# A two-phase attention and expert kernel on one core: one block in place of two, the first expert's weights loaded during the last attention, and a new order of GpSimd's pieces

## The chip, the cores and the metric

One core of a Trainium2 chip (trn2) runs the whole program. The metric is the device time of one execution in microseconds (us); the profile's span runs from the first to the last instruction of one profiled execution. The engines are TensorE (PE, its weight load PEld), VectorE (DVE), ScalarE (ACT), GpSimd (POOL) and SyncE (SP). SP, ACT and POOL issue DMAs.

## What is computed

x and ctx are 8 batches of 512 tokens with 256 features. In short:

```python
x = x + tanh(g_xattn) * cross_attention(layernorm(x), ctx, ctx)      # 16 heads of 16
u = layernorm(x)
h = u + attention(rmsnorm(u, g1), wq, wk, wv, wo)                    # causal, rotary
logits = rmsnorm(h, g2) @ w_router                                   # 8 experts, best 2 of each token
moe = sum over the 2 experts e: weight_e * (silu(r @ wg[e]) * (r @ wu[e])) @ wd[e]   # r = rmsnorm(h, g2), hidden 704
x = x + tanh(g_ffn) * (h + moe)
```

## The kernel before, in words

The program has two blocks, each with an instruction list for every engine. All engines leave the first before any begins the second.

**The first block** does both attentions of all batches and the routing. Its work is a list of 16 units (L60), a cross or an own (causal) attention of one batch, each in four groups of four heads. It is written as steps -1 to 7 (LAST is 7); a step has eight stages of 16 PE units, 128 PE units in all. In a unit of stage s, PE computes one tile of scores for the row maxima (`max_unit`, L645), one tile for the exponentials of the group before (`key_unit`, L665), and products with the values. DVE reduces the maxima (L981). At the end of a stage POOL splits the group's negated maxima into three bf16 parts (`split_neg`, L1298 on; its operations are L1305 to L1308), PE turns them in the middle of the next stage (`neg_turn`, L710), ACT sends them into the stack of queries, and the exponentials wait for that. So POOL is late when the split of a stage is not done by the middle of the next one.

Tables at L142 to L178 say at which PE unit (`at(step, unit)`) or POOL stage (`stage(step, s)`) all the rest happens: the rows of x and ctx, projections, rotary terms (`rotate`, POOL, L1315 on), the rows of h (DVE, L1112), their squares (ACT, L920), `hn2_rows` (POOL, L1344), which PE turns for the router (`turn("hn2", ...)`, L729), `choose` and `place` on DVE (L1033 to L1082), `base_rows` (POOL, L1351 and L1352: the residual with its gate, which SP stores into the output) and `scatter` (POOL, L1372 and L1374: four indirect DMAs for each of the two experts k, which put 128 rows each into `rows_in`, ordered by expert). Both scatters of a batch send the same buffer `hn2[b % 2]`, whose last column is rewritten between them, so the second waits until the first has landed. POOL also splits the experts' weights into high and low parts, in 64 pieces of 256 to 704 columns (`split_piece`, L1278 to L1282, eight for each expert), as many in each stage as `PIECES_IN_STEP` says; in a stage all but the last piece, then `hn2_rows` and `base_rows`, come ahead of `split_neg`, and the scatters and the last piece behind it.

```python
for b, k in due(ROTATE_STAGES, now): rotate(b, k)
...
for n in pieces_in(now)[:-1]: split_piece(n)
for b, _ in due(HN2_STAGE, now): hn2_rows(b)
for b, _ in due(BASE_STAGE, now): base_rows(b)
if ng: split_neg(step, ng)
...
for b, k in due(SCATTER_STAGES, now): scatter(b, k)
for n in pieces_in(now)[-1:]: split_piece(n)
```

At the end DVE makes a table (`table`, L1156 to L1187) with the expert, the first row and the weight offset of each of 71 tiles, SP stores a tile of padding behind each expert's rows (L632, eight DMAs), and SP and POOL wait until everything has landed.

**The second block** has its own buffers (L1431 on). SP loads expert 0 and, when it has landed, expert 1 (`load_expert`, L1477 and L1478, about 4.2 MB each, in four DMAs); expert e comes when expert e - 2 is used up. For each of 71 tiles of 128 rows ACT loads the rows (L1569), PE turns them (L1611), ACT and DVE make high and low parts (L1576, L1527), PE multiplies (L1634), ACT and DVE do silu and product (L1587, L1546 to L1549), PE turns that (L1647) and multiplies again (L1658), DVE scales (L1536) and POOL adds the rows into the output with an indirect DMA (L1502).

Of the kernel before, what the change touches and what calls it, by code (L numbers as in the profile page):

```python
# [13 lines left out]

# [16 lines left out]
HG = 4  # L31
# [103 lines left out]
def stage(i, s):  # L135
# [9 lines left out]
X1_SUMS = {b: at(b - 2, 124, 128) for b in BATCHES} | {0: at(-1, 112, 114), 1: at(0, 46, 48), LAST: at(LAST - 2, 112, 114)}  # L145
# [27 lines left out]
BASE_STAGE = {b: stage(b + 1, 5) for b in BATCHES} | {LAST - 1: stage(LAST, 1), LAST: stage(LAST, 5)}  # L173
SCATTER_STAGES = {b: (stage(b + 2, 5), stage(b + 2, 6)) for b in BATCHES} | \
    {LAST - 4: (stage(LAST - 2, 2), stage(LAST - 2, 3)), LAST - 3: (stage(LAST - 1, 2), stage(LAST - 1, 3)),
     LAST - 2: (stage(LAST - 1, 7), stage(LAST, 0)), LAST - 1: (stage(LAST, 4),) * 2, LAST: (stage(LAST, 7),) * 2}
PIECES_IN_STEP = {-1: (0, 0, 1, 1, 1, 1, 1, 1), 0: (2, 0, 0, 0, 1, 2, 2, 1), LAST - 2: (0, 0, 1, 2, 1, 0, 1, 1),
                  LAST - 1: (2, 0, 0, 3, 3, 2, 1, 1), LAST: (0,) * 8}  # L178
# [93 lines left out]
def flamingo_block(nc, x, ctx, g_xattn, g_ffn, wq, wk, wv, wo, w_router, wg, wu, wd, g1, g2, out):  # L272
# [25 lines left out]
    with outer:  # L298
# [23 lines left out]
        with ExitStack() as st:  # L322
# [3 lines left out]
            squares_sb = s1("squares_sb", 5, P)  # L326
# [8 lines left out]
            q_stack = [s1(f"q_stack{g}", HG, S, dt=BF16) for g in range(G)]  # L335
            k_stack = [s1(f"k_stack{g}", HG, S, dt=BF16) for g in range(G)]
            probs = s1("probs", 2, HG, S)
            v_of = {"cross": s1("v_cross", QT, H, 32), "own": s1("v_own", QT, H, 32)}
            x_in, ctx_in = s1("x_in", QT, D), s1("ctx_in", QT, D)
# [3 lines left out]
            hn1_t, flat_q, flat_k = s1("hn1_t", DC, S), s1("flat_q", DC, S), s1("flat_k", DC, S)  # L343
            turned = {"q": s1("turned_q", DC, S), "k": s1("turned_k", DC, S)}
            with_cos = {"q": s1("with_cos_q", DC, S), "k": s1("with_cos_k", DC, S)}
            rest = s1("rest", DC, S)
            parts = {"q": s1("parts_q", 3, DC, S, dt=BF16), "k": s1("parts_k", 3, DC, S, dt=BF16)}
            out_t = s1("out_t", S)
            own_t = s1("own_t", DC, S)
            kept = s1("kept_sb", 2, QT, D)  # L350
            h = s1("h", QT, D)
# [12 lines left out]
            sq, ss = s1("sq", D), s1("ss", QT)  # L364
# [9 lines left out]
            def bank(name, dt=F32, n=512):  # L374
# [16 lines left out]
                rank_r route scat tab_ld pad_at pad""".split()  # L391
# [53 lines left out]
            def values_read(eng, which, b):  # L445

                u = UNIT_OF[which, b]
                users = [n for n, unit in enumerate(UNITS[:u]) if value_tile(*unit) == value_tile(which, b)]
                if users:
                    eng.wait_ge(m["pv_mm"], (users[-1] + 1) * (G * 16))  # L450

# [3 lines left out]
            def _(sp):  # L455
# [58 lines left out]
                def load_kept(b):  # L514
                    sp.wait_ge(m["kept_st"], (b + 1) * 32)
                    over(sp, m["h_base"], b)
# [23 lines left out]
                def body(step):  # L540
# [96 lines left out]
                sp.wait_ge(m["ld_pad"], 16 * SPARE)  # L637


            @block.tensor  # L640
            def _(pe):
# [209 lines left out]
                run_steps(pe, body)  # L851


            @block.scalar
            def _(act):
# [100 lines left out]
                run_steps(act, body)  # L956


            @block.vector
            def _(dve):  # L960
                v = nc.vector
                chain = Chain(dve, m["dve"])
                v.memset(count[:, :], 0.0)
# [91 lines left out]
                def place(b, c):  # L1055
# [18 lines left out]
                    if c == 2:  # L1074
# [4 lines left out]
                        v.tensor_copy(hn2[b % 2][:, :, D:D + 1], token[:, :].rearrange("p (t e) -> p t e", e=1))  # L1079
# [61 lines left out]
                def table(v, chain):  # L1141
# [33 lines left out]

                    link(v.tensor_tensor(among, wide(full_f), passed, ALU.mult))
# [49 lines left out]
            def _(pool):  # L1226
# [467 lines left out]
```

## Time and profile before

| | us |
|---|---|
| three runs, median (lowest to highest) | 1619.45 (1614.07 to 1620.33) |
| the profiled execution's own time | 1617.12 |
| its span | 1614.5 |
| PE busy | 1441.7 (89% of the span) |
| DVE busy | 978.8 (61%) |
| POOL busy | 879.8 (54%) |
| ACT busy | 776.8 (48%) |

The share of busy time is a mean over two stages that differ. It has to be read by stretches, and at each idle stretch of PE by what ended it. A number in square brackets in a row of the timeline is the time for which the engine sat idle before that row, with what ended it.

### The profile page before, as it was taken

To read this page: it belongs to the slowest core of one execution; us is meant where nothing else is said; L and a number is where in the kernel's file an instruction comes from. 1 tells how busy PE (TensorE), PEld (TensorE's weight loads), DVE (VectorE), ACT (ScalarE), POOL (GpSimd) and SP (SyncE) were. 2 spreads that over 40 slices of the span, in tenths; PEclk is the share of its full clock that TensorE was granted. 3 is DMA by queue.
4 is the path that set the end of the run, shared out by engine and by line. 5 is a ranking of instruction groups with operands and counts; after the bars stand their busy time and mean duration, and the time that the engine had idled before them with its cause. 6 is when DMAs were issued, how large, how long until landed. Compare 5 with 4: busy or idle time off the path is not lost. (4 is left out here: it accounts for less than half of the span.)

```text
span 1614.5 us, 31714 instructions
## 1 busy us (share of the span) xinstructions
PE 1441.7 (89%) x9439; PEld 885.6 (55%) x9439; DVE 978.8 (61%) x2328; ACT 776.8 (48%) x1781; POOL 879.8 (54%) x1146
## 2 busy tenths in 40 slices
PE   3999999999999999999997997841999999999997
PEld 1232334444444444444444454431899999999996
DVE  5887757658757767757755654332555555555554
ACT  1566665665664665664664554610333333333332
POOL 7475765874876867975777686541122222222222
PEclk9899999999998999999998998955999999999999
DMA  7665365663564566564453556116343543455221
GB/s 204 175 173 176 95 187 163 177 203 117 178 205 149 157 187 190 150 224 134 141 162 98 196 147 212 55 65 238 83 138 50 147 135 86 115 148 148 40 41 14
DMA packets 116517, 230.19 MB, mean 143 GB/s; under 512 B 20101, under 2 KB 82949, under 8 KB 114310
## 3 DMA queue, kind: packets, MB, share of 16 engines
q1 hardware_dynamic: 76690, 148.18, 30.5%
q0 software_dynamic: 26032, 69.82, 15.4%
q10 hardware_dynamic: 13636, 10.18, 2.4%
q8 instruction: 86, 1.41, 0.4%
q14 instruction: 73, 0.60, 0.1%
HBM read 135.10 MB, written 93.14 MB: 141 GB/s over the span
## 5 line engine op out<-in xcount | busy, mean ns | idle before, releaser
L981 DVE TENSOR_REDUCE neg<-max_ps 128x1 f32<-128x512 f32 (+3 forms) x864 | 544.1, 666 | 304.3 <-PE max_ps L662 197.5
L867 ACT ACTIVATE probs<-key_ps 128x512 f32<-128x512 f32 (+3 forms) x1024 | 497.2, 519 | 388.5 <-PE key_ps L679 192.0
L659 PE MATMUL max_ps<-k_stack,q_stack 96*128 96x512 bf16 (+3 forms) x1024 | 360.0, 355 | 35.2 <-DVE neg L981 21.3
L676 PE MATMUL key_ps<-q_stack,k_stack 99*128 99x512 bf16 (+3 forms) x1024 | 355.5, 348 | 25.1 <-ACT probs L867 16.5
L1502 POOL DMA_INDIRECT out<-part,whose x71 | 110.7, 1559 | 390.1 <-DVE part L1536 328.7
L1634 PE MATMUL up_ps<-weights,rows_t 128*128 x1278 | 292.5, 383 | 5.8 <-DMA weights<-w_split 4.8
L1634 PEld LDWEIGHTS up_ps<-weights,rows_t 128*128 128x128 f32 x1278 | 233.4, 190 | 44.3 <-issue 6.4
L659 PEld LDWEIGHTS max_ps<-k_stack,q_stack 96*128 96x128 bf16 x1024 | 101.7, 99 | 224.0 <-DVE neg L981 116.2
L676 PEld LDWEIGHTS key_ps<-q_stack,k_stack 99*128 99x128 bf16 x1024 | 101.0, 99 | 131.4 <-ACT probs L867 69.1
L1658 PE MATMUL y_ps<-weights,hidden_t 128*128 x1207 | 160.7, 287 | 1.4 <-DVE hidden_t L1556 1.4
L1658 PEld LDWEIGHTS y_ps<-weights,hidden_t 128*128 128x128 f32 x1207 | 147.7, 189 | 1.7 <-issue 1.7
L697 PE MATMUL pv_ps<-probs,v_cross 128*32 128x512 f32 (+3 forms) x1024 | 132.4, 588 | 3.4 <-ACT out_t L937 2.3
L1597 ACT ACTIVATE hidden_t<-hid_ps 128x512 fp32r<-128x512 f32 (+1 forms) x142 | 61.9, 488 | 134.2 <-PE hid_ps L1647 134.2
L1587 ACT ACTIVATE silu<-up_ps 128x512 f32<-128x512 f32 (+1 forms) x142 | 66.0, 465 | 112.0 <-PE up_ps L1634 112.0
L1305 POOL TENSOR_SCALAR neg_parts<-neg 128x16 bf16<-128x16 f32 x64 | 16.2, 253 | 180.4 <-DVE neg L981 155.0
L679 PE MATMUL key_ps<-squares_b 128*128 128x128 bf16 x512 | 114.5, 224 | 0.0
L662 PE MATMUL max_ps<-squares_b 128*128 128x128 bf16 x512 | 113.4, 221 | 0.0
L697 PE MATMUL pv_ps<-probs,v_own 128*32 128x512 f32 (+3 forms) x1024 | 103.5, 473 | 3.1 <-ACT out_t L937 2.0
L1546 DVE TENSOR_TENSOR hidden<-silu,up_ps 128x320 f32<-128x320 f32 x71 | 34.6, 488 | 101.1 <-ACT silu L1587 101.1
L1576 ACT ACTIVATE rows_t<-rows_ps,g_sb 128x128 fp32r<-128x128 f32 x142 | 44.3, 363 | 103.9 <-PE rows_ps L1611 103.9
L1279 POOL TENSOR_TENSOR w_parts<-w_in,w_parts 128x704 fp32r<-128x704 f32 (+2 forms) x64 | 85.9, 1343 | 5.4
L1556 DVE TENSOR_TENSOR hidden_t<-hid_ps,hidden_t 128x512 fp32r<-128x512 f32 x71 | 49.1, 692 | 45.4 <-ACT hidden_t L1597 45.4
(202 smaller groups left out, 1966.0 us busy)
## 6 DMA issues: line engine op xcount, KB each, us to landing
w_split<-w_parts POOLq DMA_DIRECT2D x32, 704.0 KB, 5.6
weights<-w_split SPq DMA_DIRECT2D x8, 2816.0 KB
weights<-w_split SPq DMA_DIRECT2D x8, 1280.0 KB
rows<-rows_in ACTq DMA_DIRECT2D x71, 129.0 KB, 2.1
w_split<-w_parts POOLq DMA_DIRECT2D x16, 512.0 KB, 3.5
kept_sb<-kept SPq DMA_DIRECT2D x16, 512.0 KB, 6.2
parts_cross_k<-parts_k SPq DMA_DIRECT2D x48, 128.0 KB
parts_cross_q<-parts_q SPq DMA_DIRECT2D x48, 128.0 KB
```

What stands on the lines that cost most here:

```text
L659: r = mm(ps[:, 0:keys], q_stack[g][0:KROWS, hd, qt * P:(qt + 1) * P], k_stack[g][0:KROWS, hd, 0:keys], start=True, stop=not own)
L662: r = mm(ps[:, qt * P:keys], ident_b, mask_qk, start=False, stop=True)
L676: r = mm(ps[:, q0:S], k_stack[g][0:KROWS + NEGROWS, hd, kt * P:(kt + 1) * P], q_stack[g][0:KROWS + NEGROWS, hd, q0:S], start=True, stop=no ...
L679: r = mm(ps[:, q0:q0 + P], ident_b, mask_kq, start=False, stop=True)
L697: mm(pv_ps[32 * hd:32 * hd + 32, q0:S], v_of[value_tile(which, b)][:, kt, g * HG + hd, :], probs[:, kt % 2, hd, q0:S], start=(kt == 0), st ...
L867: act.activation(probs[:, kt % 2, hd, q0:S], key_ps[j % 2][:, q0:S], ACT.Exp).then_inc(m["exp_done"], 1)
L981: v.tensor_reduce(neg[:, g % 2, hd - place_:hd + 1, qt], scores, op=ALU.max, axis=AX.X, negate=True).then_inc(m["max_red"], many)
L1279: chain.link(g_.tensor_tensor(low, whole, high, ALU.subtract))
L1502: g_.indirect_dma_start(out=out_rows, out_offset=bass.IndirectOffsetOnAxis(ap=whose[j % OWNERS][:, 0:1], axis=0), in_=part[j % OWNERS][:, ...
L1587: act.activation(silu[:, f0:f1], chunk(j, k)[:, 0:f1 - f0], ACT.Silu).then_inc(m["silu"], 1)
L1634: r = mm(ps, rows_t[:, a, c, :], weights[:, bass.ds(off + (w_ * WALL + c * 2 * F + n0), n1 - n0)], start=(c == 0 and (a, w_) == PASSES[0]) ...
L1658: r = mm(y_ps[:, 0:D], hidden_t[:, a, k, :], weights[:, bass.ds(off + (w_ * WALL + 2 * WG + k * D), D)], start=(k == 0 and (a, w_) == PASS ...
```

## The change

- **One block.** The second block's work is made by `expert_stage()` inside the first, with the same loops; each engine goes on to it when its own list is done. Its buffers lie over attention buffers that are no longer used: the weights' two halves over the stacks, x_in, ctx_in, v_cross, flat_q and parts; silu, hidden, hidden_t and part over probs; the PSUM banks are the attention's. Waits take the place of the meeting: ACT waits for part 1 of the table (expert, row, weight offset, now computed ahead of the rest), all scatters and all padding before it loads rows; POOL waits for the base rows' stores and the whole table.
- **Expert 0** is loaded by SP right behind `load_kept(LAST)` in step 7, when the last batch but one's attention is done with its values; expert 1 when the last keys are used, expert 0 and the first four tiles' rows have landed.
- **Padding**: four of the eight stores go to ACT. `base_rows(LAST)` comes behind the last scatters instead of ahead of them, and its store behind the padding.
- **The last batch's rows** are copied to the other buffer (one POOL operation), so its second scatter needs no wait for the first. The scatters of batch LAST - 1 move from stage 4 of step 7, behind `hn2_rows(LAST)`, to stage 3, ahead of it.
- **POOL's order**: in stages 0 and 5 `hn2_rows` comes first. Pieces move: one more in step 0 stage 7; in step 5 from stages 2 to 7 (1, 2, 1, 0, 1, 1) to (2, 2, 0, 0, 2, 1); in step 6 from stages 3 to 7 (3, 3, 2, 1, 1) to (2, 1, 2, 2, 1). The second scatter of batch LAST - 3 moves from stage 3 to 4 of step 6.
- ACT has one Silu ahead of the experts, DVE's memset of the weights' unused corner moves to the program's start, and the first half of the sums for x1 moves six units forward in the regular steps.

```diff
-X1_SUMS = {b: at(b - 2, 124, 128) for b in BATCHES} | ...
+X1_SUMS = {b: at(b - 2, 118, 128) for b in BATCHES} | ...
-BASE_STAGE = {... LAST: stage(LAST, 5)}
+BASE_STAGE = {... LAST: stage(LAST + 1, 0)}
-    {... LAST - 3: (stage(LAST - 1, 2), stage(LAST - 1, 3)), ... LAST - 1: (stage(LAST, 4),) * 2, LAST: (stage(LAST, 7),) * 2}
-PIECES_IN_STEP = {-1: (0, 0, 1, 1, 1, 1, 1, 1), 0: (2, 0, 0, 0, 1, 2, 2, 1), LAST - 2: (0, 0, 1, 2, 1, 0, 1, 1),
-                  LAST - 1: (2, 0, 0, 3, 3, 2, 1, 1), LAST: (0,) * 8}
+    {... LAST - 3: (stage(LAST - 1, 2), stage(LAST - 1, 4)), ... LAST - 1: (stage(LAST, 3),) * 2, LAST: (stage(LAST, 7),) * 2}
+PIECES_IN_STEP = {-1: (0, 0, 1, 1, 1, 1, 1, 1), 0: (2, 0, 0, 0, 1, 2, 2, 2), LAST - 2: (0, 0, 2, 2, 0, 0, 2, 1),
+                  LAST - 1: (2, 0, 0, 2, 1, 2, 2, 1), LAST: (0,) * 8}
...
+                    if first:
+                        for kind in ("x", "c", "oq", "ok"):
+                            stored(sp, kind, B)
+                        sp.wait_ge(m["x_norm"], B)
+                        sp.wait_ge(m["v_cross"], B)
+                        sp.wait_ge(m["pv_mm"], 16 * G * UNIT_OF["own", LAST])
+                        load_expert(0, 0)
+                        return
+                    sp.wait_ge(m["key_mm"], 16 * G * 2 * B)
+                    for n in range(ROW_RING):
+                        sp.wait_ge(x_ld[n], 16)
+                    sp.wait_ge(t_["w_ld"], W_LOADS)
+                    load_expert(1, 1)
+                    sp.wait_ge(m["table"], 2)
...
+                    act.wait_ge(m["table"], 1)
+                    act.wait_ge(m["scat"], B * 2 * QT * 16)
+                    act.wait_ge(m["pad"], 16 * E)
+                    act.wait_ge(m["ld_pad"], 16 * SPARE)
+                    for j in range(ROW_RING):
+                        load(j)
...
                         send_base(LAST - 1)
                         load_kept(LAST)
-                        send_base(LAST)
+                        expert_sync(sp, True)
...
-                for e in range(E):
-                    at_ = sp.value_load(pad_i[0:1, e:e + 1], min_val=0, max_val=ROWS - P)
-                    sp.dma_start(rows_in[bass.ds(at_, P), :], padding[:, :]).then_inc(m["pad"], 16)
-                sp.wait_ge(m["pad"], 16 * E)
-                sp.wait_ge(m["base_st"], 16 * B)
+                end_rows(sp, 0)
+                send_base(LAST)
+                expert_sync(sp, False)
...
+                    if b == LAST:
+                        pool.wait_ge(m["h_norm"], B)
+                        pool.wait_ge(m["scat"], b * (2 * QT * 16))
+                        aux_full(pool, "hn2", b - 1, DC - 1)
+                        g_.tensor_scalar(hn2[(b + 1) % 2][:, :, 0:D], hn2[b % 2][:, :, 0:D], 1.0, 0.0, ALU.mult, ALU.add).then_inc(m["hn2_twice"], 1)
...
+                        soon = s in (0, 5)
+                        if soon:
+                            for b, _ in due(HN2_STAGE, now):
+                                hn2_rows(b)
...
                 run_steps(pool, body)
-                pool.wait_ge(m["scat"], B * 2 * QT * 16)
-                for n in range(2):
-                    pool.wait_ge(w_part_st[n], E * len(pieces) // 2 * 16)
+                base_rows(LAST)
+                expert_gpsimd(pool)
```

## Rows read from the trace of the kernel before

**Rows 1.** Windows, three stretches: length, busy time of each engine, clock, DMA share, GB/s

```profile
1040.00:1066.00 26.00, 19.32 (x118) 12.13 (x118) 6.73 (x37) 7.34 (x20) 5.43 (x5) 0.74 0.22 77
1066.00:1122.00 56.00, 7.00 (x40) 5.66 (x40) 17.92 (x67) 5.05 (x13) 24.33 (x30) 0.53 0.42 154
...
1140.00:1614.50 474.50, 464.72 (x2973) 426.01 (x2971) 252.60 (x756) 166.22 (x411) 109.28 (x71) 0.99 0.38 93
```

**Rows 2.** Timeline of PE: start, duration, line, operation, idle before it

```profile
862.10 1.11 PE L729 MATMUL aux<-ident,hn 128*128 128x128 f32 x4 [7.45 <-POOL hn L1344]
...
987.15 0.30 PE L710 MATMUL turn_ps<-squares_b,neg_parts 128*48 128x128 bf16 x1 [10.19 <-POOL neg_parts L1308]
...
1002.18 0.24 PE L710 MATMUL turn_ps<-squares_b,neg_parts 128*48 128x128 bf16 x1
...
1116.68 0.69 PE L1611 MATMUL rows_ps<-ident,rows 128*128 128x128 f32 x2 [35.44 <-DMA rows<-rows_in]
1122.17 6.27 PE L1634 MATMUL up_ps<-weights,rows_t 128*128 x18 [4.80 <-DMA weights<-w_split]
```

**Rows 3.** Timeline of POOL, stages 4 and 5 of step 5

```profile
852.03 1.41 POOL L1315 TENSOR_TENSOR turned_k<-turned_k,rope_sb 128x512 f32<-128x512 f32 x1
...
858.76 0.20 POOL L1285 TENSOR_SCALAR tmp_r<-ss 128x4 f32<-128x4 f32 x1
```

**Rows 4.** Windows behind PE's two stalls, columns as in rows 1

```profile
862.10:868.00 5.90, 5.90 (x27) 2.71 (x27) 1.38 (x2) 2.75 (x5) 5.51 (x7) 0.54 0.24 58
...
987.20:991.00 3.80, 3.80 (x22) 1.73 (x23) 1.11 (x2) 1.04 (x3) 3.42 (x4) 0.58 0.02 3
```

**Rows 5.** Timeline of POOL, stages 3 and 4 of step 6

```profile
960.21 0.19 POOL L1372 COPY hn<-weight 128x4 f32<-128x4 f32 x1
...
978.38 0.77 POOL L1278 TENSOR_SCALAR w_parts<-w_in 128x704 fp32r<-128x704 f32 x1 [2.19 <-DMA w_split<-w_parts]
...
982.75 0.19 POOL L1285 TENSOR_SCALAR tmp_r<-ss 128x4 f32<-128x4 f32 x1
...
985.99 0.21 POOL L1305 TENSOR_SCALAR neg_parts<-neg 128x16 bf16<-128x16 f32 x1
```

**Rows 6.** Timeline of ACT, the last square of batch LAST - 2

```profile
968.13 0.41 ACT L920 ACTIVATE sq<-h 128x256 f32<-128x256 f32 x1
```

**Rows 7.** Timeline of POOL at the end of the first block

```profile
1067.75 0.20 POOL L1285 TENSOR_SCALAR tmp_r<-ss 128x4 f32<-128x4 f32 x1 [21.59 <-ACT sq L920]
...
1070.96 0.19 POOL L1372 COPY hn<-weight 128x4 f32<-128x4 f32 x1
...
1083.64 1.12 POOL L1351 TENSOR_SCALAR h<-h,gate 128x1024 f32<-128x1024 f32 x1
...
1087.48 0.19 POOL L1372 COPY hn<-weight 128x4 f32<-128x4 f32 x1 [0.29 <-DVE token L1082]
...
1095.41 0.19 POOL L1372 COPY hn<-weight 128x4 f32<-128x4 f32 x1 [2.29 <-DMA rows_in<-hn,pos_i]
...
1099.95 0.97 POOL L1374 DMA_INDIRECT rows_in<-hn,pos_i  x1 [0.30 <-issue]
```

**Rows 8.** Timeline of DVE beside them

```profile
1083.14 1.64 DVE L1078 TENSOR_TENSOR mix<-mix,e_gap 128x4 f32<-128x4 f32 x1
...
1084.89 2.32 DVE L1080 TENSOR_SCALAR weight<-mix,gate 128x8 f32<-128x8 f32 x1
```

**Rows 9.** DMA issues, 1050 to 1125 us: count, KB each, us to landing

```profile
rows<-rows_in ACTq DMA_DIRECT2D x4, 129.0 KB, 9.9
```

**Rows 10.** The page's DMA issues, whole span

```profile
rows<-rows_in ACTq DMA_DIRECT2D x71, 129.0 KB, 2.1
```

**Rows 11.** Timeline of SP and ACT's queue, and the critical chain's transfer

```profile
1049.19 0.80 SPq L519 DMA_DIRECT2D kept_sb<-kept  x2
...
1107.58 3.56 ACTq L1569 DMA_DIRECT2D rows<-rows_in  x4
...
1108.61 13.44 DMA weights<-w_split
```

More of the change, by code:

```diff
@@ L13 @@
 from contextlib import ExitStack
+import math
 import numpy as np
@@ L333, in flamingo_block, with placed, next_place, inside @@
             half = s1("half", 2 * QT)
-            q_stack = [s1(f"q_stack{g}", HG, S, dt=BF16) for g in range(G)]
-            k_stack = [s1(f"k_stack{g}", HG, S, dt=BF16) for g in range(G)]
-            probs = s1("probs", 2, HG, S)
-            v_of = {"cross": s1("v_cross", QT, H, 32), "own": s1("v_own", QT, H, 32)}
-            x_in, ctx_in = s1("x_in", QT, D), s1("ctx_in", QT, D)
+            def placed(name, at, *shape, dt=F32):
+                return nc.alloc_sbuf_tensor_at(name, [P, *shape], dt, offset=at)
+            def next_place():
+                return (nc.sbuf_base + 31) // 32 * 32
+            weights_at = next_place()
+            weights = s1("weights", 2 * 2 * WALL, dt=F32R)
+            probs_at = next_place()
+            probs = s1("probs", 2, HG, S)
+            def inside(name, quarter, at, *shape, dt=F32):
+                size = math.prod(shape) * (2 if dt == BF16 else 4)
+                assert at + size <= 4 * (WALL - D)
+                return placed(name, weights_at + 4 * quarter * WALL + at, *shape, dt=dt)
+            q_stack = [inside(f"q_stack{g}", 2, g * 2 * HG * S, HG, S, dt=BF16) for g in range(G)]
+            k_stack = [inside(f"k_stack{g}", 3, g * 2 * HG * S, HG, S, dt=BF16) for g in range(G)]
+            v_of = {"cross": inside("v_cross", 0, 0, QT, H, 32), "own": s1("v_own", QT, H, 32)}
+            x_in, ctx_in = (inside(n, 0, 4 * (QT * H * 32 + k * QT * D), QT, D) for k, n in enumerate(("x_in", "ctx_in")))
             xq = s1("xq", QT, D)
@@ L390, in flamingo_block @@
                 h_sq h_rstd h_norm h_base gap_r gap_exp hot_r
-                rank_r route scat tab_ld pad_at pad""".split()
+                rank_r route scat tab_ld pad_at pad table hn2_twice""".split()
             m = {n: sem("s_" + n, st) for n in names}
@@ L956, in _ @@
                 run_steps(act, body)
+                act.activation(ss[:, 0:1], ss[:, 0:1], ACT.Silu)
+                act.wait_ge(m["pad_at"], 1)
+                end_rows(act, 1)
+                expert_scalar(act)
             @block.vector
@@ L1078, in place @@
                         chain.link(v.tensor_tensor(mix[:, 1, :], mix[:, 0, :], e_gap[:, :], ALU.mult))
-                        v.tensor_copy(hn2[b % 2][:, :, D:D + 1], token[:, :].rearrange("p (t e) -> p t e", e=1))
+                        for n in range(2 if b == LAST else 1):
+                            if n:
+                                dve.wait_ge(m["scat"], b * (2 * QT * 16))
+                            v.tensor_copy(hn2[(b + n) % 2][:, :, D:D + 1], token[:, :].rearrange("p (t e) -> p t e", e=1))
                         chain.link(v.tensor_scalar(weight[:, b % 2, :, :].rearrange("p a b -> p (a b)"),
@@ L1222, in _ @@
                 table(v, chain)
+                expert_vector(dve)
             @block.gpsimd
@@ L1369, in scatter @@
                     pool.wait_ge(m["route"], b + 1)
+                    if b == LAST:
+                        pool.wait_ge(m["hn2_twice"], 1)
                     pool.wait_ge(m["h_norm"], b + 1)
-                    over(pool, m["scat"], b * (2 * QT * 16) + k * (QT * 16))
-                    chain.link(g_.tensor_copy(hn2[b % 2][:, :, D + 1:DX], weight[:, b % 2, k, :].rearrange("p (t e) -> p t e", e=1)))
+                    rows_ = hn2[(b + (b == LAST and k)) % 2]
+                    over(pool, m["scat"], b * (2 * QT * 16) + (k * (QT * 16) if b < LAST else 0))
+                    chain.link(g_.tensor_copy(rows_[:, :, D + 1:DX], weight[:, b % 2, k, :].rearrange("p (t e) -> p t e", e=1)))
                     for t in range(QT):
@@ L1395, in body @@
                             split_piece(n)
-                        for b, _ in due(HN2_STAGE, now):
-                            hn2_rows(b)
+                        if not soon:
+                            for b, _ in due(HN2_STAGE, now):
+                                hn2_rows(b)
                         for b, _ in due(BASE_STAGE, now):
```

447 lines of the change are left out of this document (227 added, 220 removed).

## The prediction

> **What bounds the kernel now.** I read the windows first, to see where PE is not at work, then PE's timeline for what ended each long idle time, then the timeline of the engine that ended it. The reader is to see three things. The expert stage is PE alone: 464.72 of 474.5 us busy, and a tile about every 6.7 us (474.5 / 71) [rows 1]; only a shorter tile would help there, and the change leaves the tile as it is. Between the attentions and the experts PE has 7.00 us of work in 56 [rows 1], waits 35.44 us for rows and then 4.80 us for weights, and begins to multiply at 1122.17 [rows 2]. And inside the attentions, where PE is otherwise nearly full, it stands still twice because POOL is late: 7.45 us for hn2 and 10.19 us for a split of the maxima [rows 2]. Each time the granted clock is near its lower level (0.54 and 0.58 of 2.4 GHz) for some microseconds behind the stall [rows 4]. All sums below are in the profiled execution's own time.
>
> **The first stall, step 5 (7.45 us at 862.10).** POOL did a piece, the 6.7 us of a rotation (852.03 to 858.76), and then hn2 [rows 3], which PE had wanted since 862.10 - 7.45 = 854.65 [rows 2]. The change takes the piece out of stage 4 and puts hn2 ahead of the rotation. hn2 takes 862.10 - 858.76 = 3.3 us [rows 2, 3]; if it starts where the piece did, at about 848, it is done near 851.4, 3 us early. The rotation then ends near 858.1, the base rows (3.6 us, from 1083.64 to DVE's release before 1087.48 [rows 7]) near 861.7, and this stage's split 1.2 us later, in time for PE by some 1 us. The pieces go to stages 2 and 6, into waits for DVE; I cost them at nothing, and at 4.4 us each if that cover is gone (978.38 to 982.75 [rows 5]). Gain 7.45. The clock: 5.90 us of full work at 0.54 [rows 4] would be 3.2 us at full clock, so up to 2.7 us come back; ACT and DVE allow less, I take 2.0. **Term: 9.4 us** (0 to 10.2).
>
> **The second stall, step 6 (10.19 us at 987.15).** PE wanted the split at 976.96 and got it 1.2 us after POOL began it at 985.99. Ahead of it POOL had a scatter from 960.21, three pieces of stages 3 and 4 up to 982.75, and hn2 [rows 5]. The squares that hn2 needs were there at 968.13 + 0.6 = 968.7 [rows 6]. After the change only one piece stands between the split of stage 3 and hn2; so hn2 starts at 968.7, the split at 972, and PE waits for nothing. What is late next: the moved scatter (5.5 us, 1095.41 to 1100.92 [rows 7]), two pieces (2 x 4.4), base rows (3.6) and a split (1.2) follow, from 973.1 to 992.2. PE wants that split 1002.18 - 987.15 = 15.0 us after the one before [rows 2], less 1.6 us for the clock (3.80 us at 0.58 [rows 4]): at 976.96 + 13.4 = 990.4. So 1.8 us of stall are left. **Term: 10.2 + 1.6 - 1.8 = 10.0 us** (0 to 11.8).
>
> **Elsewhere in the attentions.** The extra piece of step 0, the new kinds of pieces in the stages (their numbering moves by one in steps 1 to 4) and the six units by which a sum moves stand beside waits for DVE: nothing, -3 to +2 us as bounds, the 4.4 us of a piece being the nearest row.
>
> **The border, from the last squares to the first expert product.** The chain is squares, hn2 (POOL, 1067.75 [rows 7]), router, choice (DVE), scatters (POOL), meeting of the engines, rows, product.
> - *The moved scatters.* Those of batch LAST - 1 ran behind hn2, in the time for the router. Now they come ahead of it, in POOL's 21.59 us of idle time [rows 7]. Eight DMAs of about 1.3 us and two copies take 12.7 us (1070.96 to 1083.64 [rows 7]) and would fit from 1052 on. But SP now issues 4.2 MB of weights right behind the kept rows of 1049.19 [rows 11], and that transfer took 13.44 us and the issue before it 2 [rows 11]: with the kept rows ahead of it the DMA engines are full from 1050.0 for 16.4 us, until 1066.4. Four transfers of 129 KB beside such a load landed in 9.9 us [rows 9], against 2.1 over the whole run [rows 10]. The second four scatters wait for the landing of the first, at about that time; 5.5 us later, at 1071.9, they are issued, and hn2 starts there instead of at 1067.75. Loss 4.1 us, between 0 (they land in time) and 6. I take 4.1, as rows 9 is the same size beside the same load.
> - *The base rows of the last batch* no longer run in front of the last scatters. DVE's two tiny operations took 1.64 and 2.32 us beside them [rows 8], against some 0.2 for their like; the router's answer comes 3.2 us sooner, from 1087.48 [rows 7] to 1084.3. By rule of the Trainium skill, SBUF — State Buffer, section Who interferes with whom, a DVE operation with one SBUF input outside the two-port modes is not held up by GpSimd; L1080 reads one tensor, and if its 2.32 us had another cause, 2.1 us less would come back. The trace has it end as POOL's operation ends, so I keep 3.2.
> - *The second scatter of the last batch* does not wait for the first any more (2.29 us [rows 7]). With the 3.2 the last issue ends at 1100.92 - 5.2 = 1095.7 and lands 2.3 later, at 1098.0. The added copy of 128 x 1024 on POOL (about 1.1 us, as L1351 [rows 7]) lies in the time for the router.
> - *The meeting and the block's start* go. Rows are issued 1 us after the wait (at 1099.0) instead of at 1107.58 [rows 11], and land in 2.1 us [rows 10] instead of the 9.1 up to 1116.68 [rows 2], since no weights are under way: PE turns them at 1101.1. Then 2.0 us for the turn and the high and low parts and 0.9 for PE's register loads: the first product at 1104.0, against 1122.17 [rows 2]. With the 4.1 from above it is 1108.1. The weights have been there since 1066.4, so their 4.80 us go too; without that cover they cost up to 15.4 us. The table is done earlier (it wants 6 us from the router's answer, the scatters 11), SP's and ACT's four paddings each too. The store of the last base rows (512 KB) may cross the rows: up to 2 us. SP now has expert 1 behind the rows, 60 us ahead of its use.
>
> **Term: 14.1 us** (10 to 18).
>
> **Sum.** 9.4 + 10.0 + 14.1 = 33.5 us: a span of 1581.0 and a time of 1583.6 from the profiled 1617.12. That execution is 2.3 us below the median of the three runs, 1619.45; from the median it is 1586.0, and that is my forecast. They spread over 6 us, so about 0.5% (8 us) is what a measurement of this kernel can tell from no change.
>
> **The rivals.**
> 1. *The second stall only moves* (0.17). POOL is as loaded as before between stages 4 and 6 of step 6, and my estimate has its split late by 1.8 us already. If a wait for a weights' buffer like the 2.19 us of rows 5 comes on top at each piece, most of the 10 us come back: 1595. Against it: two pieces fewer in the step.
> 2. *The scatters land in time* (0.2). The weights' load leaves them enough of the engines, or starts later: 4.1 us more, 1582.
> 3. *POOL's order is not what stops PE* (0.06). Both stalls return behind the next thing; only the border is gained: 1605. Against it: PE's row names POOL's operation both times.
> 4. *Expert 0 is not loaded early* (0.04): SP is held by one of the new waits until the table. Then rows and weights cross again: 9.9 - 2.1 = 7.8 us come back, 1594. Against it: those waits are for batches already stored.
> 5. *The tile gets longer* (0.03), the way to a slower kernel. In the expert stage every operand now lies among other buffers, the PSUM banks are others, and DVE, ACT and POOL go round with PE in a tight circle. 33.5 us are used up at 33.5 / 71 = 0.47 us a tile, and from 0.58 the kernel is slower by over 0.5%; at 0.7 it takes 1586 + 50 = 1636. Against it: the instructions, shapes and rings are the same.
>
> **How the numbers follow.** My forecast has 0.5. Its own range, with the bounds of the terms, is 1579 to 1593; rivals 1, 2 and 4 lie at 1595, 1582 and 1594. The range 1575 to 1599 leaves out rivals 3 and 5 and the far ends, some 2 in 10. Faster by over 0.5% (below 1611): all but rival 5 and what I have not thought of, 0.93; within 0.5%: 0.04; slower: 0.03.
>
> **What would show it.** In the new profile: no PE row with more than 3 us of idle time behind POOL's hn2 or split in steps 5 and 6; rows landed in about 2 us and the first product some 40 us after the last square (54.5 before); POOL's hn2 of the last batch some 4 us behind that square; DVE's L1080-like row at 0.2 us; tiles still 6.7 us apart. I am wrong if PE still waits for POOL by several us in step 6, if the product waits for weights, or if a tile takes over 6.9 us.

## The result and the profile after

The changed kernel took 1581.12 us in the median of four runs (1575.98 to 1583.01), the kernel before 1619.89 us on the same chip (1614.07 to 1621.9): a ratio of 0.9761, 95% interval 0.9727 to 0.9796, so 33 to 44 us less. I had forecast 1586.0 in 1575 to 1599. The profiled execution has a span of 1573.6 us and is the fastest of the four; a later one of the same kernel had 1582.0.

PE's timeline of the changed kernel answers to [rows 2] (start, duration, line, operation, idle before it):

```profile
591.08 0.24 PE L997 MATMUL turn_ps<-squares_b,neg_parts 128*48 128x128 bf16 x1 [2.30 <-POOL neg_parts L1607]
...
837.70 0.24 PE L997 MATMUL turn_ps<-squares_b,neg_parts 128*48 128x128 bf16 x1 [1.02 <-POOL neg_parts L1607]
...
975.00 0.30 PE L997 MATMUL turn_ps<-squares_b,neg_parts 128*48 128x128 bf16 x1 [2.97 <-POOL neg_parts L1607]
...
1047.20 1.12 PE L1016 MATMUL aux<-ident,hn 128*128 128x128 f32 x4 [8.26 <-POOL hn L1643]
...
1075.28 0.66 PE L666 MATMUL max_ps<-ident,rows 128*128 128x128 f32 x2 [17.89 <-DMA rows<-rows_in]
1078.78 1.64 PE L689 MATMUL max_ps<-weights,rows_t 128*128 x3 [2.84 <-DVE rows_t L580]
```

The reader is to see what is not there any more: the 7.45 us for hn2 in step 5, the 10.19 us for the split in step 6, and any wait for weights. What is left is 2.97 us for the next split of step 6, 1.02 us in step 5 (0.82 before), and one that is new: 2.30 us in step 3 (0.36 before). The first expert product waits 2.84 us, but for the rows' low part, not for weights.

The end of the attentions on POOL, which answers to [rows 7]:

```profile
1038.31 0.19 POOL L1679 COPY hn<-weight 128x4 f32<-128x4 f32 x1 [6.84 <-DMA rows_in<-hn,pos_i]
...
1043.88 0.20 POOL L1584 TENSOR_SCALAR tmp_r<-ss 128x4 f32<-128x4 f32 x1
...
1060.12 0.19 POOL L1679 COPY hn<-weight 128x4 f32<-128x4 f32 x1 [11.84 <-DVE token L1378]
...
1065.50 0.19 POOL L1679 COPY hn<-weight 128x4 f32<-128x4 f32 x1
...
1069.80 0.96 POOL L1681 DMA_INDIRECT rows_in<-hn,pos_i  x1 [0.30 <-issue]
```

And ACT, whose first line answers to [rows 11] and whose second says why PE waits for `rows_t`: the rows were turned at 1075.94, but ACT issued loads until 1077.22.

```profile
1073.05 4.17 ACTq L621 DMA_DIRECT2D rows<-rows_in  x4
1077.27 0.62 ACT L628 ACTIVATE rows_t<-max_ps,g_sb 128x128 fp32r<-128x128 f32 x2 [20.05 <-issue]
```

**Where the time went.** I laid the two profiled executions side by side at every turn of a split by PE (L710, now L997), 64 places. The distance is by how much sooner the changed kernel gets to the same turn. It opens to 10.4 us by step 5 stage 4. In each of steps 0 to 4 it opens by 1.9 to 3.5 us between the turns of stages 6 and 7 (and by 1.4 us once more in step 2, between stages 4 and 5), and it closes once by 3.5 us, in step 3. The first stall adds 9.7 there (9.0 are left a stage later), the second 10.2, of which 4.2 are lost within two stages. At the end of the attentions it is 25.8 us. From the last square (1067.66, now 1041.84) to the first expert product it was 54.5 us and is 36.9: 17.6 more. The expert stage and the end are 2.5 us longer (492.3 to 494.8). Sum: 25.8 + 17.6 - 2.5 = 40.9, the difference of the spans. That is this execution, the fastest of its kernel. The second profiled one (run 9 below) has 20.4 + 14.8 - 2.8 = 32.4: its stalls brought nearly the same (over their whole steps 9.2 and 5.3, against 9.2 and 6.0), the rest of its attentions 5.9 instead of 10.6, and its border with the tail 3.1 less.

So the border, with the longer tail, brought 15.1 against the 14.1 that I had said (12.0 in the second execution); the attentions brought 25.8 against 19.4 (20.4 in the second), and what was over came from a part that I had costed at nothing. What opens at the ends of the steps is seen in windows there. Before, in steps 1 to 4 (the columns are those of [rows 1]):

```profile
387.00:400.00 13.00, 11.99 (x83) 6.05 (x87) 11.53 (x24) 7.62 (x18) 9.82 (x17) 0.87 0.61 174
510.00:520.00 10.00, 8.24 (x42) 3.78 (x44) 8.99 (x21) 4.23 (x9) 5.67 (x9) 0.66 0.62 177
637.00:647.00 10.00, 9.73 (x63) 4.47 (x63) 9.05 (x20) 5.86 (x14) 7.69 (x12) 0.83 0.78 202
760.00:770.00 10.00, 9.60 (x47) 3.30 (x47) 8.19 (x19) 4.86 (x10) 7.76 (x13) 0.66 0.57 153
```

After, at the same places:

```profile
383.00:396.00 13.00, 12.01 (x97) 5.82 (x95) 12.18 (x26) 8.23 (x20) 9.22 (x16) 1.00 0.61 173
502.00:512.00 10.00, 8.44 (x69) 3.76 (x67) 9.79 (x26) 5.85 (x14) 5.25 (x9) 1.00 0.53 146
630.00:640.00 10.00, 9.01 (x68) 3.91 (x66) 9.53 (x20) 6.60 (x16) 7.50 (x11) 1.00 0.67 197
750.00:760.00 10.00, 8.57 (x67) 3.46 (x63) 9.90 (x23) 5.42 (x12) 6.78 (x10) 1.00 0.51 155
```

In the second of these windows PE's busy time hardly differs (8.24 and 8.44 us), but it does 42 matmuls in one and 69 in the other: the clock was granted at 0.66 to 0.87 of 2.4 GHz there before, and is at 1.00 after. DVE in the kernel before, in the same window, shows what went ahead of it:

```profile
508.97 0.74 DVE L1128 SCALAR_TENSOR_TENSOR x<-att_cross,gate,x 128x512 f32<-128x512 f32 x1
509.74 0.69 DVE L981 TENSOR_REDUCE neg<-max_ps 128x1 f32<-128x512 f32 x1
510.35 0.74 DVE L1132 BATCH_NORM_STATS2 st<-x 128x6 f32<-128x256 f32 x2
511.13 0.26 DVE L996 RECIPROCAL recip<-turn_ps 128x16 f32<-128x16 f32 x1
511.42 0.42 DVE L1001 TENSOR_TENSOR att_own<-turn_ps,recip 128x256 f32<-128x256 f32 x1
511.76 1.88 DVE L981 TENSOR_REDUCE neg<-max_ps 128x1 f32<-128x512 f32 x3
```

and PE with it:

```profile
512.59 0.58 PE L659 MATMUL max_ps<-k_stack,q_stack 96*128 96x512 bf16 x1 [1.53 <-DVE neg L981]
```

Four operations of DVE that are not maxima (2.2 us) follow almost on each other, PE waits 1.53 us until DVE has read the bank that its next scores go to, and then runs at the lower clock. The two sums (L1128, L1132) are what the change moves six units forward. DVE had time there: in the kernel before it was busy for 6.75 of ten microseconds up to 510, and for 9.72 of the ten up to 515.

```profile
500.00:510.00 10.00, 9.36 (x74) 4.39 (x73) 6.75 (x18) 4.65 (x13) 7.28 (x8) 1.00 0.46 144
505.00:515.00 10.00, 7.61 (x62) 3.44 (x60) 9.72 (x25) 3.53 (x10) 4.33 (x8) 0.88 0.41 130
```

DVE's share alone doesn't tell: in the windows of the changed kernel it is higher still (94 to 99%), and PE's longest wait for DVE there is 0.72 us. What counted was how the operations stood together. One pair of executions could owe the lower clock to chance, so I took the same stretch, from the turn of stage 6 to that of stage 7 in steps 0 to 4, in every trace of the runs below. With the sums at unit 124 (three traces, 15 places) PE waits 1.53 us for DVE at all 15, and the lower clock comes at 11 of them. With the sums at 118 (ten traces, 50 places) the longest wait is 0.72 us, and the lower clock comes at none. The five stretches take 80.5 to 81.6 us together with 124, and 68.1 us in the first execution of the changed kernel (69.3 in the second): 11 to 13.5 us. Where the lower clock did not follow, the 1.53 us cost 1.5 to 1.9 us; where it did, 1.9 to 3.6.

### The profile page after: what moved, and what is told of

The parts are those of the page before. It is cut to its first block, busy times and chain, and to the rows that moved or that the text cites. A ratio compares the mean times of both kernels' runs of the same rounds, so it can differ in the third digit from the quotient of the medians.

```text
span 1573.6 us, 31721 instructions
## 1 busy us (share of the span) xinstructions
PE 1433.8 (91%) x9439; PEld 881.3 (56%) x9439; DVE 975.2 (62%) x2329; ACT 777.3 (49%) x1782; POOL 879.7 (56%) x1147
## 4 chain that ended last, share of the span: by engine, by line
PE 68%; POOL 9%; DVE 8%; issue 5%; ACT 4%; DMA 4%; SPq 1%; ACTq 0%; POOLq 0%; DVEq 0%
PE pv_ps L984 9%; PE pv_ps L713 9%; PE max_ps L689 9%; PE key_ps L689 9%; PE max_ps L946 8%; PE key_ps L963 8%; DVE neg L1274 4%; PE aux L1032 3%; PE aux L1023 3%; ACT probs L1155 2%; PE turn_ps L702 2%; PE aux L1016 2%; POOL rows_in L1681 2%; DMA q_stack<-neg_rows 2%; POOL w_parts L1578 1%
## 5 line engine op out<-in xcount | busy, mean ns | idle before, releaser
L946 PE MATMUL max_ps<-k_stack,q_stack 96*128 96x512 bf16 (+3 forms) x1024 | 356.1, 352 | 30.8 <-DVE neg L1274 16.2
L963 PE MATMUL key_ps<-q_stack,k_stack 99*128 99x512 bf16 (+3 forms) x1024 | 350.3, 343 | 24.4 <-ACT probs L1155 16.0
L713 PE MATMUL pv_ps<-weights,hidden_t 128*128 x1207 | 161.9, 288 | 1.4 <-DVE hidden_t L609 1.4
L689 PE MATMUL max_ps<-weights,rows_t 128*128 x642 | 153.7, 385 | 2.8 <-DVE rows_t L580 2.8
L689 PE MATMUL key_ps<-weights,rows_t 128*128 x636 | 150.3, 381 | 1.0 <-DVE rows_t L580 1.0
L713 PEld LDWEIGHTS pv_ps<-weights,hidden_t 128*128 128x128 f32 x1207 | 149.0, 191 | 1.7 <-issue 1.7
L689 PEld LDWEIGHTS max_ps<-weights,rows_t 128*128 128x128 f32 x642 | 117.8, 191 | 22.9 <-issue 3.2
L689 PEld LDWEIGHTS key_ps<-weights,rows_t 128*128 128x128 f32 x636 | 115.1, 189 | 20.2 <-issue 1.2
L653 ACT ACTIVATE hidden_t<-turn_ps 128x512 fp32r<-128x512 f32 x71 | 42.4, 597 | 135.5 <-PE turn_ps L702 133.3
L628 ACT ACTIVATE rows_t<-max_ps,g_sb 128x128 fp32r<-128x128 f32 x142 | 44.4, 364 | 85.7 <-PE max_ps L666 65.6
L609 DVE TENSOR_TENSOR hidden_t<-turn_ps,hidden_t 128x512 fp32r<-128x512 f32 x71 | 49.1, 692 | 45.6 <-ACT hidden_t L653 45.6
```

The source lines that it names most:

```text
L609: v.tensor_tensor(lo[:, 0:4, :].rearrange("p k t -> p (k t)"), hid_ps[0][:, :], hi[:, 0:4, :].rearrange("p k t -> p (k t)"), ALU.subtract) ...
L689: r = mm(ps, rows_t[:, a, c, :], weights[:, bass.ds(off + (w_ * WALL + c * 2 * F + n0), n1 - n0)], start=(c == 0 and (a, w_) == PASSES[0]) ...
L713: r = mm(y_ps[:, 0:D], hidden_t[:, a, k, :], weights[:, bass.ds(off + (w_ * WALL + 2 * WG + k * D), D)], start=(k == 0 and (a, w_) == PASS ...
L946: r = mm(ps[:, 0:keys], q_stack[g][0:KROWS, hd, qt * P:(qt + 1) * P], k_stack[g][0:KROWS, hd, 0:keys], start=True, stop=not own)
L963: r = mm(ps[:, q0:S], k_stack[g][0:KROWS + NEGROWS, hd, kt * P:(kt + 1) * P], q_stack[g][0:KROWS + NEGROWS, hd, q0:S], start=True, stop=no ...
```

## The experiments

The first four ran beside one another on one chip, where the kernel before took 1624.6 us (median of 11). They split the change into its attention and border halves, and the attention half into the sums and POOL's order.

**1. The sums alone.** The kernel before with

```diff
-X1_SUMS = {b: at(b - 2, 124, 128) for b in BATCHES} | ...
+X1_SUMS = {b: at(b - 2, 118, 128) for b in BATCHES} | ...
```

> The kernel before with one edit: the first half of the x1 sums moved from unit 124 to 118 in the regular steps. In the two profiled executions the distance to before opens by 1.6 to 3.5 us at the end of each of steps 0, 1, 2 and 4, beside a stretch at the lower clock that the new kernel does not have. Theory A (two DVE operations come out of a crowd in which PE waits for maxima and then falls to the lower clock): 7 to 11 us faster than before, no stretch at the lower clock at the ends of these steps. Rival B (my prediction: the move costs nothing and brings nothing, the stretches at the lower clock fall where they like): within 2 us of before.

1611.44 us, ratio 0.9928 (0.9908 to 0.9947): 9 to 15 us faster. Theory A. At the ends of steps 1 to 4 its windows show the full clock, as in

```profile
511.00:521.00 10.00, 9.01 (x71) 4.14 (x69) 9.58 (x21) 6.24 (x15) 7.13 (x10) 1.00 0.60 181
```

**2. POOL's order alone.** The kernel before with the diff's lines of SCATTER_STAGES for LAST - 3, PIECES_IN_STEP and `soon`.

> The kernel before with the new order on GpSimd alone (hn2 first in stages 0 and 5, the moved pieces, the scatter of batch LAST - 3 one stage later), two blocks as before. Theory A: both stalls go but for 3 us: 15 us faster (9 to 10 in step 5, 6 in step 6). Rival (the stalls go to the next thing): under 8 us. If the sums' crowd costs more because POOL has moved, sums and order together bring more than the sum of the two alone.

1614.48 us, ratio 0.994 (0.9917 to 0.9962): 6 to 13 us faster, between the two theories. Both stalls are gone in its trace, but for 2.92 us in step 6, and it keeps the crowd at the ends of the steps (81.6 us in the five stretches, 81.3 before). But it falls behind the kernel before by 13 us up to the end of step 4. The largest part, 6.7 us, is lost in step 3 from stage 3 to 6: PE waits 2.28 us for a split there, and the lower clock follows. How much of the rest is the order's doing and how much the clock's chance, this run can't tell.

**3. Both, without the border.** The kernel before with the edits of 1 and 2.

> The kernel before with the new order on GpSimd and the moved sums, two blocks as before, so all of the change but the border. Theory A: 24 to 26 us faster than before, the last att_own turn at about 1027 us as in the changed kernel; what is then left to the changed kernel, 13 to 15 us, is the border. Rival (the border's earlier expert load or the new buffers' places also change the attentions): under 20 us.

1597.42 us, ratio 0.9839 (0.9817 to 0.9861): 23 to 30 us faster. Theory A: the attention half is two thirds to three quarters of the whole. Its two parts sum to 21 alone and bring 26 together; the intervals are too wide to say whether they help each other. Its last square comes 20.8 us sooner than before, 20.4 in the second execution of the changed kernel (25.8 in the first), so the early load and the new places of the buffers are not seen to change them.

This kernel also shows once more how POOL holds DVE. Its base rows stand ahead of the last scatters as before:

```profile
1062.28 1.80 DVE L1076 TENSOR_SCALAR mix<-e_gap 128x4 f32<-128x4 f32 x1
...
1064.33 2.16 DVE L1078 TENSOR_TENSOR mix<-mix,e_gap 128x4 f32<-128x4 f32 x1
...
1066.60 0.23 DVE L1080 TENSOR_SCALAR weight<-mix,gate 128x8 f32<-128x8 f32 x1
```

POOL, beside it:

```profile
1062.92 1.13 POOL L1351 TENSOR_SCALAR h<-h,gate 128x1024 f32<-128x1024 f32 x1
1064.13 2.34 POOL L1352 TENSOR_TENSOR kept_sb<-h,kept_sb 128x1024 f32<-128x1024 f32 x1
```

DVE's operations end as POOL's end (1064.08 and 1064.05, 1066.49 and 1066.47). In [rows 8] L1078 and L1080 were held, here L1076 and L1078: whichever is under way. L1076 has one SBUF input, and the trace has it held. The rule that I had weighed in the prediction (the Trainium skill, SBUF — State Buffer, section Who interferes with whom) spares such an operation only outside the two-port modes, and the same section counts `tensor_scalar` among the operations that can enter them. I had left that half out. It would fit L1076 and L1080; no run here shows in which mode they ran.

**4. The sums put back.** The changed kernel with 124 in place of 118.

> The changed kernel with the sums back at unit 124. Theory A: 7 to 11 us slower than the changed kernel, so 28 to 32 us faster than before. Rival B: no difference to the changed kernel.

1596.31 us, ratio 0.9834 (0.9816 to 0.9851), against 0.9761 of the changed kernel, and 0.9782 when it ran again (run 9): 8 to 12 us of its gain are this one number. The windows at the ends of its steps have the lower clock again:

```profile
515.00:525.00 10.00, 8.47 (x43) 3.67 (x42) 8.41 (x20) 4.62 (x9) 6.31 (x10) 0.66 0.67 191
```

The next four are on the border, on another chip, where the kernel before took 1621.64 us. The times of three of them differ by less than the executions of one kernel do, so they are read in the trace, from the last square to the first expert product: 54.5 us before, 36.9 in the changed kernel. But this stretch varies too, 36.4 to 39.7 us over four traces that differ only outside it (the changed kernel twice, runs 4 and 10), nearly all by how late hn2 comes. So each run is read at its own link of the chain.

**5. Expert 0 held.**

```diff
+                        sp.wait_ge(m["scat"], LAST * (2 * QT * 16))
                         load_expert(0, 0)
```

> The changed kernel, but SP begins to load expert 0 only when the scatters of batch LAST - 1 have landed. In the changed kernel the second four of these scatters wait 6.84 us for the landing of the first, and hn2 of the last batch starts 2.0 us after its squares. Theory A (the weights' load slows these scatters): the wait falls to some 2.3 us, hn2 starts at once, and from the last square to the first expert product it takes 35 us instead of 36.9; the weights still land before the rows. Rival (the scatters are slow by themselves when they follow each other in two batches): the wait stays over 5 us and nothing is gained.

34.9 us, and POOL's wait is short:

```profile
1044.08 0.19 POOL L1680 COPY hn<-weight 128x4 f32<-128x4 f32 x1 [1.78 <-DMA rows_in<-hn,pos_i]
```

Theory A. hn2 starts 0.09 us after the last square instead of 2.04. In the three traces in which no expert is loaded beside these scatters (runs 5, 7 and 11) POOL waits 1.8 to 1.9 us for their landing, in the six with the early load 6.0 to 7.3. The window shows the cause: while it loads, the DMA engines are full.

```profile
1026.00:1041.00 15.00, 9.74 (x24) 6.49 (x24) 2.06 (x5) 2.42 (x7) 6.01 (x8) 0.50 0.99 377
```

(That is the changed kernel: DMA share 0.99, 377 GB/s.) Over all the traces with the early load hn2 came 1.2 to 4.75 us late. The whole run, 1588.22 us (0.98, 0.9749 to 0.9851), is too uncertain to show 2 us.

**6. The first rows at once.**

```diff
-                    for j in range(ROW_RING):
+                    load(0)
+                    rows(0)
+                    for j in range(1, ROW_RING):
                         load(j)
-                    rows(0)
```

> The changed kernel, but ACT issues the first tile's load, waits for its rows and makes their high part, and issues the other three loads behind that. In the changed kernel the high part of tile 0 began at 1077.27 us, when the four issues had ended, though PE had turned the rows at 1075.94. Theory A: the first product comes 1.3 us sooner. Rival (PE's register loads are what it waits for, as I wrote in the prediction: 0.9 us): under 0.5 us sooner. Later tiles may wait for their rows: up to 3 us lost again in tiles 1 to 3.

From ACT's first load to the first product 4.5 us instead of 5.7: 1.2 sooner, and no later wait for the rows (the tail is 494.3 us, not longer). Theory A: from PE's turn of the rows to the product it took 2.2 us, so the 0.9 us that I had put down to PE's register loads was hardly needed. From the last square it took 37.3 us all the same, as hn2 came 2.8 us late and ACT's first load 0.8 us later than in the changed kernel. The whole: 1585.45 us, 0.9783 (0.976 to 0.9806).

**7. Expert 0 late.** `load_expert(0, 0)` behind the padding and the last base rows' store.

> The changed kernel with expert 0's load put behind the padding and the last base rows' store, where its old place was, still without a meeting of the engines. It says what the early load brings by itself. Theory A (both the rows and the weights are then late, as in my fourth rival): rows land in 9 to 10 us instead of 2.2 and the first product waits for the weights, 54.5 - 36.9 = 17.6 us less the 4 to 6 us that the meeting alone cost, so 10 to 13 us slower than the changed kernel, and 2 us back because the scatters aren't slowed. Rival (it was the meeting that cost, the load is short enough to hide behind the rows): under 5 us slower.

46.75 us, 9.8 more, and 1596.06 us (0.9848, 0.9825 to 0.987):

```profile
1096.45 3.78 PE L689 MATMUL max_ps<-weights,rows_t 128*128 x8 [13.99 <-DMA weights<-w_split]
```

In part Theory A: the weights are waited for, but the rows had landed after 2.2 us, as they were asked for just before the load got going. It was 9.8 us, just under the range of 10 to 13. Against run 5, where the scatters aren't slowed either, the early load by itself is worth 46.75 - 34.94 = 11.8 us. The rest of the border, 54.5 - 46.75 = 7.8 us, is mostly the shorter way from hn2 to the last scatter's issue (33.2 us before, 26.9 here). The meeting is 1.6 us of it: both here and before the product waits for the weights, and SP issues them 4.1 us behind the last scatter's issue instead of 5.7; then 15.6 and 15.5 us pass up to the product.

**8. The base rows first.** `LAST: stage(LAST, 5)` in BASE_STAGE again, without the call at the end.

> The changed kernel with the base rows of the last batch ahead of the last scatters again. Theory A (GpSimd's two-input operation holds DVE's tiny operations): DVE's L1376-like operation takes about 2 us instead of 0.22 and the router's answer comes 3 us later; the first product comes 3 to 3.6 us later. Rival (by the rule on operations with one input, only the two-input operation is held): 1.5 us later, and L1376 stays at 0.2 us. Rival 2: POOL is idle from 1048.3 to 1060.1 us in the changed kernel; if base rows at stage 5 fit wholly into that idle time, nothing is lost at all.

37.3 us, 0.4 more and within what the stretch varies by; from hn2 to the router's answer 16.2 us, as in the changed kernel. DVE's weights took 0.22 us, and POOL still stood idle:

```profile
1073.70 0.19 POOL L1679 COPY hn<-weight 128x4 f32<-128x4 f32 x1 [8.33 <-DVE token L1378]
```

Rival 2. The base rows now end long before DVE's small operations, because the scatters of batch LAST - 1 are no longer ahead of them. So with the scatters moved, the 3.2 us that I had given to the move of the base rows come without it. Whether the move of the base rows alone would bring them too was not run. 1586.78 us (0.9782, 0.9742 to 0.9822).

Runs 9 to 11 ran on one chip, where the kernel before took 1620.84 us.

**9. The changed kernel once more.**

> The changed kernel once more, beside the next two on the same chip. Its first profiled execution was its fastest of four and had only three short stretches at the lower clock inside the attentions, where five others of its kind had five to seven. If those stretches are the difference, this one has more of them and a span of 1577 to 1583 us; its ratio to before stays within 0.973 to 0.980.

1585.45 us, 0.9782 (0.9759 to 0.9805), as expected: seven stretches at the lower clock inside the attentions against three. Its span is 1582.0 us, and 7 of the 8.4 us by which that is over the first one are there by step 5. In windows of 200 us from the start, the first profiled execution of the changed kernel had

```profile
0.00:200.00 200.00, 164.98 (x803) 57.66 (x804) 152.31 (x288) 104.66 (x203) 132.15 (x190) 0.99 0.58 165
200.00:400.00 200.00, 187.37 (x1323) 86.29 (x1321) 139.72 (x297) 122.60 (x275) 143.50 (x205) 1.00 0.58 176
```

and this one

```profile
0.00:200.00 200.00, 164.17 (x809) 57.94 (x813) 153.10 (x290) 105.47 (x205) 132.97 (x190) 0.97 0.58 165
200.00:400.00 200.00, 187.65 (x1293) 85.49 (x1285) 135.14 (x288) 119.90 (x268) 139.12 (x198) 0.97 0.57 174
```

So a part of what differs between executions is the clock, on the same instructions. At 219 us PE waits 1.84 to 2.07 us for a load of keys in the kernel before and in both of these; only in this one the lower clock came behind it. Nor does each stretch have a wait ahead of it: at 362.6, 608.4 and 731.3 us here PE had been idle for less than 0.3 of the five microseconds before.

**10. One piece later.**

```diff
-    count = lambda n: PIECES_IN_STEP.get(n // 8, (0, 0, 0, 2, 3, 2, 1, 0))[n % 8]
+    count = lambda n: PIECES_IN_STEP.get(n // 8, (0, 0, 0, 2, 2, 3, 1, 0))[n % 8]
...
-                  LAST - 1: (2, 0, 0, 2, 1, 2, 2, 1), LAST: (0,) * 8}
+                  LAST - 1: (2, 0, 0, 2, 1, 1, 3, 1), LAST: (0,) * 8}
```

> The changed kernel with one piece moved from stage 4 to 5 in steps 1 to 4, and in step 6 from stage 5 to 6. It tests two steps of my prediction: that PE still waits some 2 us for a split in step 6 (2.97 measured), and that the new kinds of pieces in the stages cost nothing (PE waits 2.30 us in step 3 stage 4, where it waited 0.36 before). Theory (POOL's load ahead of those splits is what PE waits for): both waits go, 3 to 7 us faster than the changed kernel. Rival (the splits of stages 5 and 6 are late instead): new waits behind POOL there, within 2 us.

1578.2 us, 0.9744 (0.9718 to 0.9769). Of the waits of PE for a split only one of 0.81 us is left, in step 5; those of steps 1 to 3 and 6 are gone, as the theory has it. Against run 9 that is 7 us less, though the intervals overlap by a little. In step 6 nothing is gained: 4.8 us are still given back behind the second stall, 3.3 in run 9. In step 3 it is 3.6 us better than run 9. Two rows of POOL say what the wait of step 3 was, the first of the kernel before, the second of the changed kernel:

```profile
602.33 0.80 POOL L1268 DMA_DIRECT2D w_in<-in_L_ffn_wd  x1 [2.00 <-issue]
585.10 0.79 POOL L1567 DMA_DIRECT2D w_in<-in_L_ffn_wd  x1 [2.04 <-issue]
```

It is the 79th of POOL's DMAs in both, and it stands 2.0 us at its issue in all 13 traces, for no cause that they show. Before, it came behind the split of that stage (PE turned it at 597.88). With one piece more in step 0 it comes ahead of the split (turned at 591.08), which is late by it; so only step 3 has this wait of 2.3 us, while steps 1 and 2, whose eight pieces are of the same kinds, have 0.5 us. In run 10 it is behind the split again. Its trace can't place the rest, as the profiled execution is only 1.0 us shorter than that of run 9 and has lost the 3.6 us again by the end of the attentions.

**11. All three edits.**

> The changed kernel with the three edits that the runs so far point to: the pieces moved as in the run above, expert 0's load held for the scatters of batch LAST - 1 (2.0 us at the border), the first tile's rows made at once (1.2 us). Theory: the three add up, 6 to 10 us faster than the changed kernel, from the last square to the first product in 33.7 us or so. Rival: the starts of the tiles that wait for later loads give the 1.2 us back, and the clock's stretches hide the rest: under 4 us.

The edits of runs 5, 6 and 10 together: **1577.94 us, 0.9733 (0.9717 to 0.9749), the fastest of all the kernels here**, and by 7.5 us faster than the changed kernel beside it, whose interval it does not touch. That is the theory's 6 to 10 us. From the last square to the first product it takes 34.2 us, 33.7 were expected. Its gain over run 10 alone is within the uncertainty.

## Why the prediction was right, and where it was not

- **The bound and the first stall.** POOL's hn2 was what PE waited for, and it went as worked out: 9.7 us, of which 0.7 were given back a stage later; the term was 9.4, and over the whole step it was 9.2 in both executions.
- **The second stall.** The wait went and the next split was late, as said: 2.97 us against 1.8. Two things were missed. There are two stretches at the lower clock around this wait, one that begins 4 us before it, with PE busy for 5.88 of the six microseconds ahead, and one behind it:

```profile
962.00:968.00 6.00, 5.88 (x60) 4.27 (x57) 2.97 (x7) 2.95 (x7) 5.53 (x6) 1.00 0.53 137
968.00:971.50 3.50, 3.50 (x19) 1.05 (x18) 3.36 (x17) 1.49 (x4) 3.12 (x4) 0.52 1.03 337
971.50:975.00 3.50, 0.53 (x6) 0.23 (x3) 2.24 (x4) 0.96 (x3) 3.24 (x6) 0.99 0.74 274
975.00:978.50 3.50, 3.50 (x19) 1.37 (x20) 1.12 (x2) 1.04 (x3) 3.12 (x5) 0.52 0.59 181
```

  And the first DMA of the moved scatter stood 2.43 us at its issue without a cause in the trace, and so in every trace with the new order on POOL. It is the 155th of POOL's DMAs. In the kernel before the 155th is the load of a piece in the same step (970.62), and it stands 2.25 us, so that was there to be read. The term was 10.0, measured 6.0 (5.3 in the second execution).
- **"Elsewhere in the attentions ... nothing".** This step failed, in both directions. I had looked for what the moved sums would stand beside, not for what they left. DVE is 61% busy over the span, and I read that as room; at the ends of the steps it is 82 to 91% busy, PE waits 1.5 us there for a bank, and with the lower clock up to 3.6 us come of it. Run 1 shows 12 us for it and run 4 8 to 12, as much as the first stall brought or more, and more than the second. And the moved numbering of the pieces cost some 3.5 us in step 3: not by their kinds, but by a stand of 2.04 us at one of POOL's DMA issues, which it put ahead of a split (run 10). I had said nothing for both together, with -3 to +2 as bounds.
- **The moved scatters.** The mechanism was right (run 5), the size 2.0 instead of 4.1 in the first execution and 4.75 - 0.09 = 4.7 in the second. I had taken the second four to start when the load ends; they started 2.5 us before its end in one and 1.4 before it in the other, and the load itself ended 1.0 us ahead of the last square in one and 0.5 us behind it in the other (worked out from the DMA share of each microsecond).
- **The base rows.** A right size, but the owner was not theirs alone: the moved scatters bring it without them (run 8). From hn2 to the router's answer it took 19.7 us and now 16.2: 3.5 against 3.2.
- **The last scatters.** From the answer to the last issue it took 13.5 us and now 10.7: 2.8 against 2.0.
- **The meeting.** From the last scatter's issue to the first load of rows 6.66 us became 2.3, where I had worked out 3.3; the landing up to PE's turn 9.1 became 2.2, as worked out; and the last part 5.5 became 3.5, where I had 2.9: ACT's issues stood in front (run 6). All links together brought 17.6 us, against 14.1, and the tail took 2.5 of them back.
- **The tail.** POOL's indirect DMAs follow each other by 6.712 instead of 6.698 us in the mean, 1.0 us over all, and from the end of the last one's issue to the end of the span it is 6.7 instead of 5.4 us. That was no term of mine; what makes it is open. Run 3, in two blocks, has 6.698 and 5.4, so both come with the single block. Rival 5, a slower tile, is ruled out.
- **The forecast.** 1586.0 against 1581.12: 33.5 us against 38.8. The two stalls and the border were forecast at 33.5 and measured at 30.3 (9.2, 6.0, 15.1); the sums, less the pieces, and the clock's chance made up 10.6. In the second execution it was 9.2, 5.3, 12.0 and a rest of 5.9, 32.4 in all. A part of the nearness is luck: the second stall brought 4 us less than its term, and a part that I had at nothing brought more than that.

## What to carry to other kernels

Where one engine is full, look at its neighbours in windows of ten microseconds, not over the span, and then at the order of their operations: an engine at 61% held PE up at the end of each of five steps, and moving two small operations by six units brought 8 to 12 us. On PE such a wait can cost more than its length: 1.53 us cost 1.5 to 3.6, by whether the lower clock followed. When an operation is moved, cost the place that it leaves as well as the one that it comes to. And a transfer that is put into idle time fills the DMA engines for everybody: a small one on the critical path beside it has to go first.

## What was not expected of the hardware

- A wait of PE of 1.5 us was followed by the lower clock (0.66 over ten microseconds) at 11 of 15 places, where I had looked for it only behind waits of 7 and 10 us; and other stretches at the lower clock had hardly any idle time ahead of them (run 9).
- The same program at the same places got the lower clock in one execution and not in another (0.97 and 1.00 over 200 us), with a difference in span of 8.4 us, of which most is there by step 5.
- Two DMA issues of POOL, the 79th and the 155th in order, stood 2.00 to 2.04 and 2.25 to 2.43 us in all 13 traces, whichever transfer they were, against 0.3 us for their like. The cause is open.
- A one-input operation of DVE on 128 x 4 values took 1.80 us beside an operation of GpSimd, 0.17 without it.
